# The signal that starts the key loads, sent 32 instructions in front of TensorE's instruction-block border

## What is computed

```python
feat = concatenate([qe, k, qe - k, qe * k], axis=-1)   # qe: the query, repeated for its 200 keys
h = feat @ W1 + b1                                      # 512 -> 64
h = where(h >= 0, h, alpha[0] * h)
a = (h @ W2 + b2)[..., 0]                               # 64 -> 1
a = where(mask == 0, -1e9, a)
w = softmax(a, axis=-1)
return einsum('bl,bld->bd', w, k)                       # 2048 x 128
```

## Time and profile before

| | |
|---|---|
| median of three runs | 917.49 us |
| the profiled execution's own time | 906.77 us |
| its span, first to last instruction | 905.1 us |
| mean granted TensorE clock | 0.988 |
| TensorE (PE) busy | 801.2 us, 89% |
| VectorE (DVE) busy | 751.3 us, 83% |
| GpSimd (POOL) busy | 658.3 us, 73% |
| ScalarE (ACT) busy | 446.2 us, 49% |
| DMA | 222.46 MB, mean 246 GB/s |

### The profile page before, as it was taken

How to read it: one execution, slowest core, us unless ns; L and a number is a source line. 1 busy time by engine, 2 the same in 40 slices (tenths; PEclk the granted TensorE clock), 3 DMA queues, 4 the chain that set the end, 5 groups by cost and what they waited for, 6 DMA issues and landing times.

```text
span 905.1 us, 55310 instructions
## 1 busy us (share of the span) xinstructions
PE 801.2 (89%) x25216; PEld 592.5 (65%) x25216; DVE 751.3 (83%) x887; ACT 446.2 (49%) x1281; POOL 658.3 (73%) x401
## 2 busy tenths in 40 slices
PE   1779989988999999898999988899999899899995
PEld 0547766666667667666667766666776667676674
DVE  4889888887888889788988888889998789898870
ACT  0345545545555555444555544455555455554551
POOL 2668877758777777776778877777887767887761
PEclk9799999999999999999999999999999999999999
DMA  8866888776788788767888886888888588887820
GB/s 238 328 246 198 263 269 259 252 242 227 245 278 260 254 257 292 227 194 252 260 264 278 278 261 194 264 265 279 284 271 288 175 269 277 269 294 246 262 60 12
DMA packets 85449, 222.46 MB, mean 246 GB/s; under 512 B 27360, under 2 KB 35552, under 8 KB 85216
## 3 DMA queue, kind: packets, MB, share of 16 engines
q1 hardware_dynamic: 85216, 218.93, 74.3%
HBM read 214.57 MB, written 4.33 MB: 242 GB/s over the span
## 4 chain that ended last, share of the span: by engine, by line
PE 76%; issue 10%; DVE 10%; ACT 3%; DMA 1%; SPq 1%; POOL 0%; POOLq 0%; DVEq 0%; ACTq 0%
PE hP L175 43%; PE poolP L175 22%; PE scoreP L175 11%; DVE keysT L530 6%; ACT act L472 3%; DVE act L538 3%; DMA keys<-in_r_q 1%; DVE logits L545 1%; DVE keysT L583 0%; SPq L321 0%; SPq L318 0%; SPq L319 0%; POOL pool_w L454 0%; DVE neg_max L551 0%; DVE biast L586 0%
## 5 line engine op out<-in xcount | busy, mean ns | idle before, releaser
L472 ACT ACTIVATE act<-hP,biast 128x200 f32<-128x200 f32 x1024 | 371.7, 425 | 289.6 <-PE hP L175 288.7
L175 PE MATMUL hP<-keysT,weff 32*64 32x200 f32 x16384 | 453.5, 339 | 57.1 <-issue 35.9
L530 DVE STREAM_TRANSPOSE keysT<-keys 128x1536 f32<-128x1536 f32 (+1 forms) x256 | 469.0, 1832 | 0.0
L175 PEld LDWEIGHTS hP<-keysT,weff 32*64 32x64 f32 x16384 | 329.3, 132 | 146.7 <-issue 99.1
L538 DVE TENSOR_TENSOR act<-hP,act 128x400 f32<-128x400 f32 x512 | 282.9, 562 | 116.7 <-ACT act L472 102.8
L415 POOL TENSOR_TENSOR weff<-qX,wp 128x1024 f32<-128x1024 f32 x128 | 243.8, 1905 | 107.0 <-PE hP L175 91.3
L419 POOL TENSOR_TENSOR weff<-weff,wk 128x1024 f32<-128x1024 f32 x128 | 305.5, 2387 | 10.0
L175 PE MATMUL poolP<-keys,pool_w 128*16 128x128 f32 x6400 | 239.1, 273 | 17.1 <-issue 15.8
L175 PEld LDWEIGHTS poolP<-keys,pool_w 128*16 128x16 f32 x6400 | 194.9, 97 | 46.1 <-issue 20.7
L454 POOL TENSOR_TENSOR pool_w<-probs_k,own_b 128x400 f32<-128x400 f32 x128 | 111.5, 872 | 119.0 <-DMA probs_k<-probs_scratch 109.7
L175 PE MATMUL scoreP<-act,w2win 128*16 128x200 f32 x2048 | 140.0, 342 | 4.5 <-DVE act L538 4.0
(11 more groups left out here) (35 smaller groups left out, 29.6 us busy)
## 6 DMA issues: line engine op xcount, KB each, us to landing
keys<-in_r_k SPq DMA_DIRECT2D x256, 576.0 KB, 5.2
keys<-in_r_k SPq DMA_DIRECT2D x128, 448.0 KB, 5.1
probs_scratch<-expd SPq DMA_DIRECT2D x32, 100.0 KB, 3.8
masks<-in_r_mask SPq DMA_DIRECT2D x128, 12.5 KB
probs_k<-probs_scratch SPq DMA_DIRECT2D x128, 12.5 KB
out_rows<-pooled SPq DMA_DIRECT2D x128, 8.0 KB
keys<-in_r_q SPq DMA_DIRECT2D x4, 256.0 KB, 5.1
act<-in_L_rec_W SPq DMA_DIRECT2D x4, 128.0 KB, 6.4
```

The source lines that it names most:

```text
L175: return t_.matmul(*args, **flags)
L472: a_.activation(act[:, h % ABUF, a, :], hP[:, 2 * (p % HSETS) + a % 2, 0:L], ACT.Identity, bias=biast[:, n, k, a:a + 1], scale=slope).then ...
L530: v_.transpose(keysT[:, n % TBUF, j0 * D:j1 * D], keys[:, n % SLOTS, j0 * D:j1 * D]).then_inc(keysT_done, 1)
```

## The change

```diff
+BEHIND = -32
...
-            waits, sent, blocks, step = 0, BLOCK_AT, 0, (0, 0)
+            waits, sent, blocks, step = 0, BLOCK_AT - BEHIND, 0, (0, 0)
```

## The result

The changed kernel takes 1026.8 us (median of 4 runs, 1020.59 to 1028.12) against 915.6 us of the kernel before (4 runs, 910.19 to 918.95). The ratio is 1.121, 95% interval [1.113, 1.128]: slower by 111 us. The forecast was 1000 us, +82 us. The two profiled executions lie 121 us apart, since the one of the kernel before was faster than its median.

What follows compares the result with a forecast made beforehand. PE was taken to bound the kernel, with waits for late instruction packets. 144 - 52 - 10 = +82 us on the profiled 906.8 us gave 989, and 10.7 us to the median 1000; forecast's own range 960 to 1090, overall 895 to 1110.

Steps and rivals of the forecast that it cites:

- What bounds the kernel: PE sets the time; its matmuls wait on "issue" for 52.2 us, at block borders where an instruction packet is late.
- The signal's time and what it passes: Keys come 0.45 us earlier against PE's request for its next packet; the packet's lead of 0.3 us becomes 0.15 us lag.
- What a stall does next: With the signal in front of the border, a stall no longer holds the keys back, so one stall makes the next.
- The price of one collision: An instruction packet waits behind one key load; two neighbouring stalls make 2.15 us, 1.07 us per block.
- How many: Three in four of the 180 signals that carry key loads collide, at 1.07 us each: 144 us.
- The list of signs: Profile expected after: PE's "issue" waits near 200 us, more than 100 of them, mean above 1 us; PE busy hardly changed.
- What goes away: PE's present "issue" stalls of 52.2 us are inside the new number: -52 us.
- other waits: PE's waits for DVE and ACT, 19.7 us, shrink while PE stands: -10 us (bounds 0 and -20).
- the packet stays ahead: Rival, chance 0.13: keys' tail ends 0.45 us earlier, no new key gets in front; faster, 891 or 865 us.
- no change: Rival, chance 0.09: leads and tails trade evenly, or PE does not wait for the fetch; 908 to 927 us.
- collisions stay single: Rival, chance 0.14: a stalled block recovers, only a third of the signals collide; +38 us, 955 us.
- Both loads in front: Rival, chance 0.08: the packet waits for both loads of a block, 2.15 us per block; +228 us, 1145 us.

Runs made afterwards that it cites:

- 128 in front: The changed kernel with its signals 128 instructions in front of the point used in the kernel before; 1000.0 us, ratio 1.088 to the kernel before.
- the cut loads: Key loads cut to 320 KB from the eleventh tile on: 866.2 us on the kernel before, 954.7 us on the change.
- the split loads: Each key load issued as two DMAs of about half its size: 949.7 us on the kernel before, 978.8 us on the change.
- the tiny DMA: The changed kernel with a DMA of 128 single numbers issued ahead of the keys at each signal; 1249.1 us, ratio 1.353 to the kernel before.
- the cut change: The changed kernel with each key load cut to 320 KB from the eleventh tile on; 954.7 us, ratio 1.031 to the kernel before.

## Why the prediction was right, and where it was off

**What bounds the kernel** held: "issue" is the late instruction packets, and the whole of PE's new idle time went there.

**The signal's time and what it passes** held in part: the keys came forward by about the 0.45 us, and came in front of the packet once a stall was there. The transfers that SP's plan moves cost nothing (ratio 0.999).

**What a stall does next** held and was the main thing: 0.74 against 0.18. What I didn't foresee is that the first collision is not more frequent than before (0.28 against 0.30). The shift of 0.45 us is in the traces (issue to asking 0.27 to 0.73 us), but the lead it was taken from was larger than 0.3 us: with keys that flow 0.9 us after their issue, some 0.2 us of it are left after a free border, and there is no lag. The expected fault at every early signal isn't there; the sequence makes the loss.

**The price of one collision** is where the working was wrong in its parts, and its size came out near by luck. I let the packet wait for one load, 3.3 us after the issue; it mostly waits for both, 4.3 us in the stall shown above and 4.4 at the median of 71 stalls with another at the next border. I had the issue 0.1 us behind the border's arrival; it stands 0.2 us in front of it at the median, 0.5 in the stall shown. And I gave PE 3.6 us for a block; in the stall shown it needed 4.1 us (323.56 to 327.65), 4.1 at the median too, since it starts slowly after a stall: 48 of the first layer's matmuls took 1.57 us there, where 63 took 1.54 us before. Two neighbouring stalls add up to -0.5 + 4.3 + 2.2 - 4.1 = 1.9 us in the case shown (0.41 + 1.49), and to -0.2 + 4.4 + 2.3 - 4.1 = 2.4 us by the medians; the median of such sums was 2.41. I had 0.1 + 3.3 + 2.35 - 3.6 = 2.15: 1.1 us too little for the loads, most of it made up for by the other two. The mistake came from the earlier trace rows: there only one load had been issued, so its trace could not tell one from all. By the Trainium skill, page "DMA: Bandwidth & Descriptors", section "Queues, rings and completion order", an engine changes queues only after a whole packet of descriptors. That this is one load at most, as I read it against the two-load price, isn't borne out: 1.00 MB of keys passed before the instruction packet. Whether one such packet can hold both loads no run shows. With the wait for both loads put into the working as it stood, the sum would have been +228 us, twice what came.

**How many**: 135 collisions were forecast, 103 waits came, 95 of them at a block border. 144 us were forecast for them, 129.4 came: fewer and longer, two errors that nearly cancel. The list of signs had "near 200 us", which its own sum doesn't give, and the range began at 960, where its lower bound of +34 us gives 951.

**What goes away** (-52) held as a term; **other waits** fell by 3.6 us, not 10.

**The term that was missing** is the clock: some +33 us of matmuls at 1.2 GHz, in none of my rivals, where the prediction had "PE busy hardly changed". It is most of what carries the result past +82: the traces have 77 us of idle time and 43 of busy time, 121 in all, and the medians 111.

Of the rivals, "the packet stays ahead" is excluded by the 129 us of "issue", "no change" by the result, and "collisions stay single" by the counts of neighbours. "Both loads in front" was nearer in its mechanism than the forecast and wrong in its sum of +228 us: its 135 stalls of 2.15 us are 103 of 1.26.

## What to carry to other kernels

In a kernel like this, a signal that starts bulk transfers should stand behind the point at which its own engine may stall for instructions. Then a stall delays the transfers too, and the distance is kept; in front of it, the transfers run ahead and make the next stall. Before a move of half a microsecond, look at what the moved thing passes and what holds it back when the engine stands, not only at the time it gains. Add to the price of TensorE's stalls the stretch at half clock that follows the longer ones.

## What the runs showed that I had not expected

- An instruction packet asked for behind key loads that flow already waits until these are nearly through, also for two loads of 320 KB (3.3 us after the issue) or of 576 and 448 KB (4.3 us). What was issued just before the asking doesn't hold it: at 307.95 it came behind one load of two. Smaller DMAs did not let it in between those that flowed.
- From an instruction packet's start to PE's going on after a stall it is 2.34 us at the median, the same within 0.03 us in the traces of the kernel before, the change, 128 in front, the cut loads, the split loads and the tiny DMA.
- In these four traces, the longer the stalls were on average, the more of the time the granted clock was at 1.2 GHz, and their number doesn't explain it: the cut change had 117 border stalls of 0.79 us and 11.1 us at half clock, 128 in front 130 of 0.92 us and 33.9 us, the change 96 of 1.30 us and 96.7 us, the one with the tiny DMA 133 of 2.04 us and 247.8 us. No run changes the stalls' length alone.
